# Making the bf16 pieces of a hidden layer inside PSUM, with TensorE doing the subtractions

## The chip, the cores and the metric

The kernel runs on one core of one Trainium2 chip. The metric is the device time of one execution in microseconds (us). Engines are named as in the profile: PE (TensorE matmuls; PEld are its weight loads), DVE (VectorE), ACT (ScalarE), POOL (GpSimd) and SP (SyncE, which issues most DMAs).

## The reference

One layer of a graph network over N = 12500 nodes (32 features: 8 scalars and 8 vectors of 3) and E = 412500 edges, sorted by destination. Cut to what matters:

```
h1 = relu(emb @ fc1_w1 / sqrt(K1)); w  = h1 @ fc1_w2 / sqrt(16)   # K1 = 10 inputs, 16 hidden units, 512 weights per edge
h2 = relu(emb @ fc2_w1 / sqrt(K1)); w2 = h2 @ fc2_w2 / sqrt(16)   # 16 hidden units, 384 weights per edge
s_t, v_t = products of w with x[src], x[dst] and the edge's direction, summed over 16 inputs
scal, gates, vecs = products of w2 with s_t, v_t, summed over 8 or 16 inputs
out = concat(tanh(scal), vecs * tanh(gates)) * norm
x = layernorm(x + segment_sum(out, dst))
```

## The kernel before, in words

An fp32 product is made on TensorE out of bf16 pieces: a number is split into three bf16 pieces (the rounded value, the rounded rest, the rest of that), and six products of pieces are stacked along the contraction. The hidden layer needs this split for each tile: `hid_parts` holds, per edge and layer, the slots 0, 1, 2 (first piece, three times), 3 and 4 (second piece, twice) and 5 (third piece), 16 values each. A DMA transpose (`turn_hid`) brings them into `hid_t`, which is the stationary operand of the products that fill `pw` with edge weights.

The work goes in 403 periods of 1024 edges (8 tiles of 128 edges; the edges of a period stand in 128 partitions by 8 columns). It is a software pipeline written out by hand: in each period every engine runs one body, in a fixed order, on five neighbouring stages called zero (two periods ahead), one, two, three and four. Period by period:

- PE: `fill(two, 1)`, `scalar_sums_turned`, `out_sums(four)` (16 transposes that add up products), `hidden(zero)` (8 matmuls, emb to hidden layer), `fill(two, 2)`, `dst_rows_made(one)` (8 matmuls that pick destination rows), `four_sums_turned` (`gates_t`, `osum_t` turned back), 4 transposes of `vector_sums`, `fill(two, 3)`, the other 20 (`vector_sums_rest`), `fill` 4 and 5, `scalar_sums`, `fill` 6, `scatter`, `vector_sums_turned`, `fill(one, 0)`, `gate_sums`. Seven `fill`s of 8 matmuls each use two halves of `pw` in turn, so a `fill` waits until DVE has multiplied what stood in its half.
- DVE: the products of the weights with node data out of PSUM into `prods`, one after another; between them small steps, `q_first` (line 1386) among them, which waits for ACT's `osum`.
- ACT: copies out of PSUM, the first bf16 pieces, `tanh_out` and `out_sums_back` (`osum`), one-hot rows.
- POOL: eight indirect gathers of source rows per period with small vector steps between them, and the two subtractions of the hidden split, `hid_less_first` and `hid_less_second`.

Each engine's order is fixed by its `body`; the engines wait for each other by semaphores. `hid_ps` (the hidden layer, 256 fp32 columns) and `xd_ps` (destination rows) share the PSUM bank `ph`. Before the change a hidden layer goes PE `hidden` (1015) -> ACT `hidden_out` (787: relu, scaled, into SBUF `hid`) -> ACT `hidden_first` (801) -> POOL `hid_less_first` (643) -> ACT `hidden_second` (807) -> POOL `hid_less_second` (648) -> SP transposes in the next period. No PE instruction waits for any of the pieces except by way of the DMA transposes.

Of the kernel before, what the change touches and what calls it, by code (L numbers as in the profile page):

```python
# [31 lines left out]
def build_gnn_layer(nc, x, src, dst, emb_t, vec, weight, fc1_w1, fc1_w2, fc2_w1, fc2_w2, out):  # L32
# [19 lines left out]
    c1 = 1.0 / (4.0 * 32.0 ** 0.5)  # L52
    c2 = 1.0 / (4.0 * 4.0)
# [42 lines left out]
    with ExitStack() as ctx:  # L96
# [29 lines left out]
        hid = sb("hid", [P, 2 * G, H])  # L126
        hid_rest = sb("hid_rest", [P, 2 * G, H])
# [75 lines left out]
        hid_ps = ph[:, 0:G * 2 * H].rearrange("p (t h) -> p t h", h=2 * H)  # L203
# [58 lines left out]
        hid_done = sem("hid_done")  # L262
        hid_a = sem("hid_a")
        hid_rest_done = sem("hid_rest_done")
# [297 lines left out]
        def _(pool):  # L562
# [13 lines left out]
            nc.gpsimd.tensor_tensor(halves[:, :], identity[:, 0:P // 2], identity[:, P // 2:P], ALU.add).then_inc(s_const, 1)  # L576

# [61 lines left out]
            def hid_less_first(a):  # L639

                pool.wait_ge(hid_a, a.n(1, 1))
                wait(pool, hid_c, a.n())
                nc.gpsimd.tensor_tensor(hid_rest[:, :, :], hid[:, :, :], hid_parts[:, a.par, :, 0:H],
                                        ALU.subtract).then_inc(hid_rest_done, 1)

            def hid_less_second(a):
                pool.wait_ge(hid_b, a.n(1, 1))
                nc.gpsimd.tensor_tensor(hid_parts[:, a.par, :, KH - H:KH], hid_rest[:, :, :],
                                        hid_parts[:, a.par, :, 3 * H:4 * H], ALU.subtract).then_inc(hid_c, 1)

# [26 lines left out]
            def program(is_general):  # L677
                def body(at, i):
# [19 lines left out]
                    if zero is not None:  # L698
                        gathers(zero, 0, (2,))
                        hid_less_first(zero)  # L700
                        gathers(zero, 0, (3,))
                    if three_on is not None:
                        emb_less_second(three_on)
                    if zero is not None:
                        gathers(zero, 0, (4,))
                        hid_less_second(zero)
# [21 lines left out]
        def _(act):  # L728
# [31 lines left out]
            def rows_of(a, side, is_general):  # L760
                if side == 1 and not is_general:
                    act.wait_ge(xd_mm, a.n(1, 1))
                    return xd_ps
# [18 lines left out]
            def hidden_out(a, beside):  # L782
                act.wait_ge(hid_mm, a.n(1, 1))
                if beside is not None:
                    act.wait_ge(xd_mm, beside.n(1, 1))
                wait(act, hid_rest_done, a.n())
                nc.scalar.activation(hid[:, :, :].rearrange("p (l t) h -> p t l h", l=2),
                                     hid_ps.rearrange("p t (l h) -> p t l h", l=2), ACT.Relu,
# [797 lines left out]
```

## Time and profile before

| | us |
|---|---|
| median of 3 runs | 6066.6 |
| lowest and highest | 6059.2, 6067.06 |
| span of the profiled execution, first to last instruction | 6434.2 |

The page of the profile gives for the profiled execution its span alone; no own time beside it is recorded. It is longer than the timed runs by 367.6 us. The busy shares are PE 92%, PEld 88%, DVE 91%, POOL 77%, ACT 62%. A period lasts from one instruction of line 1292 to the next. How to read it: two engines stand above 90%, and the rest of their time is waits for each other, so that the order of events inside one period says more than the shares.

### The profile page before, as it was taken

The page shows a single profiled execution, that of the slowest core. Times are in us where ns is not written, and L with a number is a line of the kernel's source. Part 1 is how long each engine was busy: PE and PEld are TensorE (multiplying, and loading weights), DVE is VectorE, ACT ScalarE, POOL GpSimd, SP SyncE. Part 2 cuts the span into 40 slices and gives each one's busy share as a digit, 9 for nine tenths or more (in the row PEclk, how much of TensorE's full clock was granted, in tenths as well). Part 3 has the DMA queues.
Part 4 walks back from the last instruction along what each step waited for, and adds up shares of the span by engine and source line. Part 5 has one row for each costly group of instructions (what it writes and reads, how often), then busy time and mean ns, then how long its engine had stood idle before and what let it go on. Part 6 is the DMA issues. An engine that isn't in the chain of part 4 may idle for free. (4 is left out here: it accounts for less than half of the span.)

```text
span 6434.2 us, 221220 instructions
## 1 busy us (share of the span) xinstructions
PE 5895.3 (92%) x68616; PEld 5688.0 (88%) x68616; DVE 5884.2 (91%) x7326; ACT 3993.5 (62%) x12507; POOL 4974.7 (77%) x6875
## 2 busy tenths in 40 slices
PE   4999999999999999999999999999999999999997
PEld 3898989889999988988999889889989899999997
DVE  7899999999999998989999989999999899999998
ACT  5666666666666666666666666666666566666663
POOL 6777777777778777877877778777878778787884
PEclk9999999999999999999999999999999999999998
DMA  5444444444444444444444444444444444444442
GB/s 144 89 87 85 88 91 87 86 88 89 87 88 91 86 88 88 89 86 85 92 87 87 87 85 91 86 86 88 92 86 92 85 86 93 86 93 87 92 88 54
DMA packets 1671119, 569.93 MB, mean 89 GB/s; under 512 B 1535146, under 2 KB 1619083, under 8 KB 1670536
## 3 DMA queue, kind: packets, MB, share of 16 engines
q1 hardware_dynamic: 1567911, 516.43, 36.8%
q0 software_dynamic: 103168, 53.03, 6.0%
q8 instruction: 18, 0.29, 0.0%
q14 instruction: 22, 0.18, 0.0%
HBM read 302.19 MB, written 7.26 MB: 48 GB/s over the span
## 5 line engine op out<-in xcount | busy, mean ns | idle before, releaser
L1043 PE MATMUL p<-identity,prods 128*128 128x128 f32 x29016 | 3580.0, 276 | 157.1 <-issue 81.0
L654 POOL DMA_INDIRECT nodes<-x_rows,idx x3224 | 3104.0, 963 | 704.7 <-issue 615.1
L1043 PEld LDWEIGHTS p<-identity,prods 128*128 128x128 f32 x29016 | 3219.4, 143 | 185.0 <-issue 163.6
L1038 PE MATMUL pw<-w_stack,hid_t 128*128 128x128 bf16 x22568 | 1679.3, 220 | 229.6 <-issue 110.8
L1038 PEld LDWEIGHTS pw<-w_stack,hid_t 128*128 128x128 bf16 x22568 | 1435.3, 99 | 316.6 <-issue 138.9
L1292 DVE TENSOR_TENSOR prods<-pw,V 128x2048 f32<-128x2048 f32 x403 | 922.6, 2289 | 177.2 <-remote 83.3
L1337 DVE TENSOR_TENSOR prods<-pw,M 128x1024 f32<-128x1024 f32 x806 | 975.9, 1211 | 15.9 <-issue 6.7
L1347 DVE TENSOR_TENSOR prods<-pw,VT 128x1536 f32<-128x1536 f32 x403 | 704.8, 1749 | 59.7 <-remote 53.2
L870 ACT ACTIVATE off_hot<-node_iota,off_base 128x42 f32<-128x42 f32 x3216 | 747.1, 318 | 0.0
L1314 DVE TENSOR_TENSOR prods<-pw,S 128x1024 f32<-128x1024 f32 x403 | 490.0, 1216 | 84.6 <-PE pw L1038 76.0
L610 POOL TENSOR_TENSOR vr<-V,r 128x384 f32<-128x384 f32 x403 | 347.5, 862 | 244.9 <-issue 185.5
L1322 DVE TENSOR_TENSOR prods<-pw,S 128x1024 f32<-128x1024 f32 x403 | 490.5, 1217 | 11.7 <-PE pw L1038 4.9
L1306 DVE TENSOR_TENSOR prods<-pw,S 128x1024 f32<-128x1024 f32 x403 | 490.5, 1217 | 11.6 <-remote 11.6
L738 ACT ACTIVATE emb_parts<-emb_rest 80x128 bf16<-80x128 f32 x403 | 124.9, 310 | 603.0 <-POOL emb_rest L631 388.0
L1299 DVE TENSOR_TENSOR prods<-pw,V 128x1024 f32<-128x1024 f32 x403 | 489.0, 1213 | 0.0
L1330 DVE TENSOR_REDUCE sv<-prods 128x64 f32<-128x1024 f32 x403 | 486.9, 1208 | 0.0
L751 ACT ACTIVATE off_row<-dstb,row_shift 126x1024 bf16<-126x1024 int32 x403 | 459.3, 1140 | 0.1
L845 ACT ACTIVATE th<-p 128x128 f32<-128x128 f32 x403 | 111.7, 277 | 543.2 <-PE p L1125 538.3
L598 POOL TENSOR_TENSOR msg<-th,late 128x128 f32<-128x128 f32 x403 | 164.0, 407 | 359.4 <-issue 185.0
L757 ACT ACTIVATE hot_t<-off_row 126x1024 bf16<-126x1024 bf16 x403 | 425.4, 1055 | 0.1
L813 ACT ACTIVATE vs_t<-p 128x256 f32<-128x256 f32 x403 | 154.4, 383 | 426.3 <-PE p L1043 339.5
L801 ACT ACTIVATE hid_parts<-hid 128x768 bf16<-128x768 f32 x403 | 347.0, 861 | 0.0
(136 smaller groups left out, 8242.5 us busy)
## 6 DMA issues: line engine op xcount, KB each, us to landing
dstb<-in_dst SPq DMA_DIRECT2D x403, 504.0 KB
nodes<-x_rows,idx POOLq DMA_INDIRECT x3224
emb_stack<-emb_parts SPq DMA_DIRECT2D x2418, 20.0 KB
emb<-in_emb_t SPq DMA_DIRECT2D x403, 40.0 KB
hid_t<-hid_parts SPq DMA_TRANSPOSE x806
idx<-in_src SPq DMA_DIRECT2D x403, 4.0 KB
xw<-x SPq DMA_DIRECT2D x403, 7.9 KB
vecs<-in_vec SPq DMA_DIRECT2D x403, 12.0 KB
```

Of the source, the lines that this page charges most:

```text
L654: nc.gpsimd.indirect_dma_start(nodes[:, p, t, side, :], None, x_rows, bass.IndirectOffsetOnAxis(ap=idx[:, p, side, t:t + 1], axis=0)).then ...
L870: nc.scalar.activation(off_hot[:, t, :], node_iota[:, :], ACT.Square, bias=off_base[:, t:t + 1]).then_inc(off_hot_done, 1)
L1038: mm = nc.tensor.matmul(pw[:, slot, t, :], hid_t[:, layer, a.par, t, :], w2_stack[:, lo:lo + W], start=True, stop=True)
L1043: return nc.tensor.matmul(out, column, identity[:, :], start=first, stop=last, is_transpose=True)
L1292: nc.vector.tensor_tensor(prod_v01.rearrange("p u k t w -> p k t u w"), wts.unsqueeze(1).broadcast_to([P, 2, G, 2 * C, C]), V[:, p, 0:2, : ...
L1299: nc.vector.tensor_tensor(prod_v2.rearrange("p u t w -> p t u w"), wts, V[:, a.par, 2, :, :].unsqueeze(3).broadcast_to([P, G, 2 * C, C]), ...
L1306: nc.vector.tensor_tensor(prod_s[:, :, 0, :, :].rearrange("p u t w -> p t u w"), weights(a, 1, ring).rearrange("p t (u w) -> p t u w", w=C ...
L1314: nc.vector.tensor_tensor(prod_c, weights(a, 2, ring).rearrange("p t (w u) -> p t w u", w=C), S[:, a.par, :, 0:2 * C].unsqueeze(2).broadca ...
L1322: nc.vector.tensor_tensor(prod_s[:, :, 1, :, :].rearrange("p u t w -> p t u w"), weights(a, 3, ring).rearrange("p t (u w) -> p t u w", w=C ...
L1330: nc.vector.tensor_reduce(sv[:, :, :], prod_c, AX.X, ALU.add).then_inc(sv_done, 1)
L1337: nc.vector.tensor_tensor(prod_g[:, :, half, :, :].rearrange("p u t w -> p t u w"), weights(a, 4 + half, ring).rearrange("p t (u w) -> p t ...
L1347: nc.vector.tensor_tensor(prod_o[:, :, 0:3, :, :].rearrange("p u k t w -> p k t u w"), wts.unsqueeze(1).broadcast_to([P, 3, G, C, C]), VT[ ...
```

## The change

The scaled relu output `hid` in SBUF and its rest `hid_rest` are gone. The hidden layer stays in PSUM (`hid_ps`, now ordered by layer and tile) until its three pieces are made:

- ACT `hidden_first` reads PSUM, with relu and a scale of 1 - 2^-8, and writes slots 0 to 2.
- PE `hidden_less(zero, 0)` multiplies slot 0 by minus the identity (`minus_bf`) and adds it to `hid_ps` (one matmul of 256 columns).
- ACT `hidden_second` reads PSUM again, for slots 3 and 4; PE `hidden_less(zero, 1)` subtracts slot 3; ACT `hidden_third` reads what is left, for slot 5.
- POOL's two subtractions go. The factor 1/sqrt(K1) moves into `c1` and `c2`.
- Since a matmul that starts a sum and one that continues it now meet in the bank `ph`, `dst_rows_made(one)` moves ahead of `hidden(zero)` on PE, both wait for `hid_c` of the layer before, and ACT reads `xd_ps` after `hidden` is done: `row_scalars(one, 1)` and `row_vectors(one, 1)` stand right behind `tanh_out`, then `hidden_first`, then `out_sums_back`.

```diff
+            def hid_of(copies):
+                return hid_ps.unsqueeze(2).broadcast_to([P, 2 * G, copies, H])
+            def hidden_first(a):
+                act.wait_ge(hid_mm, a.n(1, 1))
...
+                nc.scalar.activation(parts_of(a)[:, :, 0:3, :], hid_of(3), ACT.Relu, scale=below).then_inc(hid_a, 1)
             def hidden_second(a):
-                act.wait_ge(hid_rest_done, a.n(1, 1))
...
+                act.wait_ge(hid_less, a.n(2, 1))
+                nc.scalar.activation(parts_of(a)[:, :, 3:5, :], hid_of(2), ACT.Relu, scale=below).then_inc(hid_b, 1)
+            def hidden_third(a):
+                act.wait_ge(hid_less, a.n(2, 2))
+                nc.scalar.activation(parts_of(a)[:, :, 5, :], hid_ps, ACT.Relu).then_inc(hid_c, 1)
...
             def hidden(a, is_general):
                 p = a.par
                 pe.wait_ge(stack_in[p], a.k(16 * PIECES))
-                wait(pe, hid_done, a.n())
-                if not is_general:
-                    wait(pe, sv_copied, a.n(4, -6))
+                wait(pe, hid_c, a.n())
...
+            def hidden_less(a, piece, made, is_general):
+                pe.wait_ge(made, a.n(1, 1))
+                slot = (0, 3)[piece]
+                nc.tensor.matmul(hid_ps, minus_bf[:, :], hid_parts[:, a.par, :, slot * H:slot * H + H], start=False,
+                                 stop=True, skip_group_check=True).then_inc(hid_less, 1)
...
                     if two is not None:
                         vector_sums(two, four)
                         pe.wait_ge(pss_done, two.n(1, 1))
                         fill(two, 3, at.par)
+                    if zero is not None:
+                        hidden_less(zero, 0, hid_a, is_general)
+                    if two is not None:
                         vector_sums_rest(two)
...
                         fill(three, 6, at.par)
+                    if zero is not None:
+                        hidden_less(zero, 1, hid_b, is_general)
                     if four is not None:
                         scatter(four, is_general)
```

PE before, from the turned scalar sums (first row) to `fill` 4 and 5 (last row) of one period:

```order
L1092 MATMUL p<-halves,st_t 128x64
L1043 MATMUL p<-identity,prods 128x128 x16
L1015 MATMUL ph<-w_stack,emb_stack 128x32 x8
L1038 MATMUL pw<-w_stack,hid_t 128x128 x8
L1026 MATMUL ph<-xw,hot_t 128x32 x8
L1123 MATMUL p<-identity,gates_t 128x128
L1125 MATMUL p<-identity,osum_t 128x128 x2
L1043 MATMUL p<-identity,prods 128x128 x4
L1038 MATMUL pw<-w_stack,hid_t 128x128 x8
L1043 MATMUL p<-identity,prods 128x128 x20
L1038 MATMUL pw<-w_stack,hid_t 128x128 x16
```

PE now, the same place:

```order
L1079 MATMUL p<-halves,st_t 128x64
L1030 MATMUL p<-identity,prods 128x128 x16
L1013 MATMUL ph<-xw,hot_t 128x32 x8
L994 MATMUL ph<-w_stack,emb_stack 128x2x16 x8
L1025 MATMUL pw<-w_stack,hid_t 128x128 x8
L1110 MATMUL p<-identity,gates_t 128x128
L1112 MATMUL p<-identity,osum_t 128x128 x2
L1030 MATMUL p<-identity,prods 128x128 x4
L1025 MATMUL pw<-w_stack,hid_t 128x128 x8
L1002 MATMUL ph<-hid_parts,minus_bf 128x256
L1030 MATMUL p<-identity,prods 128x128 x20
L1025 MATMUL pw<-w_stack,hid_t 128x128 x16
```

The destination rows (1026, now 1013) went ahead of the hidden layer and of `fill` 2, and the first subtraction (1002) stands between `fill` 3 and the 20 transposes.

ACT before, from `tanh` to the second pieces, with the semaphores that each waits for:

```order
L845 ACTIVATE th<-p 128x128 [waits msg_done,four_back]
L787 ACTIVATE hid<-ph 128x8x2x16 [waits hid_rest_done,xd_mm,hid_mm]
L850 ACTIVATE osum<-p 128x256 [waits msg_done,four_back]
L771 ACTIVATE S<-ph 128x8x8 [waits xd_mm,pc_done,psv_done]
L801 ACTIVATE hid_parts<-hid 128x16x48 [waits turned_in11,turned_in01,hid_done]
L745 ACTIVATE row_shift<-dstb,row_node 126x1 [waits off_row_done,dstb_in1]
L813 ACTIVATE vs_t<-p 128x256 [waits vs_back,vs_sum]
L807 ACTIVATE hid_parts<-hid_rest 128x16x32 [waits hid_rest_done]
```

ACT now, the same place:

```order
L827 ACTIVATE th<-p 128x128 [waits msg_done,four_back]
L758 ACTIVATE S<-ph 128x8x8 [waits xd_mm,hid_mm,pc_done,psv_done]
L364 REGISTER_ALU
L765 ACTIVATE V<-ph 128x24x8 [waits xd_mm,hid_mm,vr_done,pv_done]
L782 ACTIVATE hid_parts<-ph 128x16x48 [waits turned_in11,turned_in01,hid_mm]
L832 ACTIVATE osum<-p 128x256 [waits msg_done,four_back]
L731 ACTIVATE row_shift<-dstb,row_node 126x1 [waits off_row_done,dstb_in1]
L795 ACTIVATE vs_t<-p 128x256 [waits vs_back,vs_sum]
L785 REGISTER_ALU
L786 ACTIVATE hid_parts<-ph 128x16x32 [waits hid_less]
```

`osum`, which stood second behind `tanh`, now stands behind S, V and the first pieces; V came forward from behind the row squares; `hidden_first` is the fourth.

## Rows read from the trace of the kernel before

**Rows 1.** The page, busy time (share of the span) and instructions of each engine.

```profile
PE 5895.3 (92%) x68616; PEld 5688.0 (88%) x68616; DVE 5884.2 (91%) x7326; ACT 3993.5 (62%) x12507; POOL 4974.7 (77%) x6875
```

**Rows 2.** Windows: stretch, busy us (instructions) of each engine, granted clock, DMA.

```profile
3000.00:4500.00 1500.00, 1398.49 (x16316) 1350.78 (x16314) 1380.33 (x1728) 942.26 (x2976) 1176.80 (x1630) 0.99 0.43 88
```

**Rows 3.** Line 1292: count, duration min/median/max in ns, first and last start.

```profile
L1292 DVE TENSOR_TENSOR prods<-pw,V x403: 2272/2292/2293, 83.8 to 6363.8; 128x2048 f32<-128x2048 f32 x135
```

**Rows 4.** Waits, 3000 to 4500 us: us in total, times, longest.

```profile
PE pw L1038 <- DVE prods L1299: 25.8, 47, 1.1
...
DVE p L1386 <- ACT osum L850: 16.9, 44, 1.0
...
ACT th L845 <- PE p L1125: 127.8, 96, 2.0
```

**Rows 5.** Timeline of one period, DVE: start us, us, line and operation.

```profile
4468.84 2.29 DVE L1292 TENSOR_TENSOR prods<-pw,V 128x2048 f32<-128x2048 f32 x1 [0.88 <-remote]
4471.05 1.22 DVE L1299 TENSOR_TENSOR prods<-pw,V 128x1024 f32<-128x1024 f32 x1
...
4474.99 0.35 DVE L1386 TENSOR_TENSOR p<-osum,p 128x192 f32<-128x192 f32 x1
...
4483.36 2.29 DVE L1292 TENSOR_TENSOR prods<-pw,V 128x2048 f32<-128x2048 f32 x1 [0.26 <-PE pw L1038]
```

**Rows 6.** Timeline of the same period, PE matmuls.

```profile
4469.30 1.94 PE L1043 MATMUL p<-identity,prods 128*128 128x128 f32 x16
...
4471.08 0.62 PE L1015 MATMUL ph<-w_stack,emb_stack 96*128 96x32 bf16 x8
...
4472.32 0.62 PE L1038 MATMUL pw<-w_stack,hid_t 128*128 128x128 bf16 x8 [0.62 <-DVE prods L1299]
...
4472.78 0.61 PE L1026 MATMUL ph<-xw,hot_t 126*128 126x32 bf16 x8
4473.24 0.31 PE L1123 MATMUL p<-identity,gates_t 128*128 128x128 f32 x1
...
4474.04 0.61 PE L1038 MATMUL pw<-w_stack,hid_t 128*128 128x128 bf16 x8
4474.48 2.35 PE L1043 MATMUL p<-identity,prods 128*128 128x128 f32 x20
...
4484.16 0.28 PE L1043 MATMUL p<-identity,prods 128*128 128x128 f32 x1
```

**Rows 7.** Timeline of the same period, ACT.

```profile
4473.86 0.28 ACT L845 ACTIVATE th<-p 128x128 f32<-128x128 f32 x1 [1.34 <-PE p L1125]
...
4474.04 0.38 ACT L787 ACTIVATE hid<-ph 128x256 f32<-128x256 f32 x1
...
4474.30 0.39 ACT L850 ACTIVATE osum<-p 128x256 f32<-128x256 f32 x1
...
4474.56 0.25 ACT L771 ACTIVATE S<-ph 128x64 f32<-128x64 f32 x1
4474.67 0.87 ACT L801 ACTIVATE hid_parts<-hid 128x768 bf16<-128x768 f32 x1
...
4481.10 0.32 ACT L778 ACTIVATE V<-ph 128x192 f32<-128x192 f32 x1
...
4481.31 1.05 ACT L757 ACTIVATE hot_t<-off_row 126x1024 bf16<-126x1024 bf16 x1
```

**Rows 8.** Groups by line, 3000 to 4500 us: count, busy us, mean ns, idle before.

```profile
L801 ACT ACTIVATE hid_parts<-hid 128x768 bf16<-128x768 f32 x96 | 82.7, 861 | 0.0
...
L813 ACT ACTIVATE vs_t<-p 128x256 f32<-128x256 f32 x96 | 36.8, 383 | 96.4 <-PE p L1043 78.9 <-issue 17.5
```

**Rows 9.** Groups of POOL by line, the same stretch: its two subtractions.

```profile
L643 POOL TENSOR_TENSOR hid_rest<-hid,hid_parts 128x256 f32<-128x256 f32 x96 | 65.7, 685 | 1.7
L648 POOL TENSOR_TENSOR hid_parts<-hid_rest,hid_parts 128x256 bf16<-128x256 f32 x96 | 65.4, 681 | 2.1 <-issue 0.3
```

More of the change, by code:

```diff
@@ L50, in build_gnn_layer @@
     assert FULL >= 8 and NS <= 512 and SCAN <= 4 and 3 * ER <= ACC
-    c1 = 1.0 / (4.0 * 32.0 ** 0.5)
-    c2 = 1.0 / (4.0 * 4.0)
+    c1 = float(K1) ** -0.5 / (4.0 * 32.0 ** 0.5)
+    c2 = float(K1) ** -0.5 / (4.0 * 4.0)
+    below = 1.0 - 2.0 ** -8
     r3 = 3.0 ** 0.5
@@ L125, in build_gnn_layer @@
         row_node = sb("row_node", [ROWS, 1])
-        hid = sb("hid", [P, 2 * G, H])
-        hid_rest = sb("hid_rest", [P, 2 * G, H])
+        minus_bf = sb("minus_bf", [P, P], BF16)
         hid_parts = sb("hid_parts", [P, 2, 2 * G, KT], BF16)
@@ L780, in row_vectors @@
                                      ).then_inc(sv_copied, 1)
-            def hidden_out(a, beside):
-                act.wait_ge(hid_mm, a.n(1, 1))
[L784 to L788, printed above, removed]
-                                     scale=float(K1) ** -0.5).then_inc(hid_done, 1)
@@ L797, in hidden_first @@
                     wait(act, turned_in[layer][a.par], a.before(2).k(16))
-                if i_first(a):
+                if a.static and a.b * 2 + a.d == 0:
                     act.wait_ge(parts_zero, 1)
-                parts = hid_parts[:, a.par, :, 0:KH].rearrange("p a (g h) -> p a g h", h=H)
-                nc.scalar.activation(parts[:, :, 0:3, :], hid[:, :, :].unsqueeze(2).broadcast_to([P, 2 * G, 3, H]),
-                                     ACT.Copy).then_inc(hid_a, 1)
+                nc.scalar.activation(parts_of(a)[:, :, 0:3, :], hid_of(3), ACT.Relu, scale=below).then_inc(hid_a, 1)
@@ L949, in body @@
                         tanh_out(four)
+                    if one is not None:
+                        row_scalars(one, 1, is_general)
+                        row_vectors(one, 1, is_general)
                     if zero is not None:
-                        hidden_out(zero, None if is_general else one)
+                        hidden_first(zero)
                     if four is not None:
                         out_sums_back(four)
-                    if one is not None:
-                        row_scalars(one, 1, is_general)
-                    if zero is not None:
-                        hidden_first(zero)
                     if turning is not None:
@@ L967, in body @@
                         scalar_sums_out(two)
+                    if zero is not None:
+                        hidden_third(zero)
                     if turning is not None:
                         off_rows(turning)
-                    if one is not None:
-                        row_vectors(one, 1, is_general)
-                    if turning is not None:
                         hot_rows(turning)
@@ L1162, in body @@
                         out_sums(four)
+                    if one is not None and not is_general:
+                        dst_rows_made(one)
                     if zero is not None:
@@ L1167, in body @@
                         fill(two, 2, at.par)
-                    if one is not None and not is_general:
-                        dst_rows_made(one)
                     if four is not None:
@@ L1192, in body @@
                         fill(three, 6, at.par)
+                    if zero is not None:
+                        hidden_less(zero, 1, hid_b, is_general)
                     if four is not None:
```

35 lines of the change are left out of this document (11 added, 24 removed).

## The prediction, made before the changed kernel ran

> **What bounds the kernel now.** I read the page's busy shares first, then one long stretch, then who waits for whom, and last one period in order of time. The shares put PE at 92% and DVE at 91%, POOL at 77%, ACT at 62% [rows 1]: two engines are near their limit, and neither is the one that the change relieves. In the stretch from 3000 to 4500 us there are 96 periods, and DVE is busy 1380.33 us of 1500, which is 14.38 us per period; the clock is granted at 0.99, the full 2.4 GHz level [rows 2]. The first product of a period runs 403 times, from 83.8 to 6363.8 us [rows 3]: 402 periods in 6280.0 us, 15.62 us each in the profiled execution, with 83.8 us ahead and 70.4 us behind (6434.2 - 6363.8). If head and tail are the same without the profiler, the timed 6066.6 us leave 5912.4 us, or 14.71 us a period: 0.33 us above DVE's busy time. I work out a period and add the difference 402 times to the median; the profiled execution's own span would move by the same amount.
>
> The waits say how PE and DVE hold each other. PE waits for the third product of DVE (line 1299) in 47 of 96 periods; DVE waits for ACT's `osum` in 44; ACT waits in all 96, 1.33 us each, for PE's turned sums before `tanh` [rows 4]. For the order I take a period close to the timed ones: 14.52 us from product to product, 4468.84 to 4483.36 [rows 5]. PE starts `hidden` at 4471.08, is through with it some 0.46 us later (8 matmuls like those of the destination rows, 4472.78 to 4473.24), and then stands until DVE's product ends (4471.05 + 1.22 = 4472.27), starting `fill` 2 at 4472.32 with 0.62 us of idle before it [rows 6]. From there it has no gap: `gates_t` is turned at 4473.24, the 20 transposes start at 4474.48, and `out_sums` of the next period at 4484.16 [rows 6]. DVE has no wait at `q_first`: it starts at 4474.99, while ACT's `osum` ends at 4474.30 + 0.39 = 4474.69 [rows 5, 7]. So DVE sets this period, and PE has some 0.6 us to spare, all of it in one place.
>
> **The change part by part.**
> POOL loses two subtractions, 0.685 + 0.681 = 1.37 us a period [rows 9]. POOL is idle nearly a quarter of the time [rows 1], and no engine of the two that bound waits for these pieces within the period. Worth 0. The transposes read the pieces a period later, so a third piece that comes somewhat earlier or later is hidden too.
>
> ACT swaps `hid` (0.38 us) and the first pieces from SBUF (861 ns for 768 elements [rows 8]) for the first pieces from PSUM, and gets a third piece of 256 elements. ACT is busy 62%; its total hardly moves, worth 0. What counts is one duration: `tanh` takes 0.28 us for 128 elements [rows 7] and `vs_t` 383 ns for 256, both out of PSUM [rows 8], 0.83 ns for each further element, so 768 elements give 0.383 + 512 x 0.00083 = 0.81 us. The SBUF row (861 ns) is the upper bound; the bare 768 x 0.83 ns, 0.64 us, the lower. I take 0.81, which goes by the rows that read PSUM.
>
> PE gets two matmuls of 256 bf16 columns. A `fill` of 8 x 128 columns takes 4474.48 - 4474.04 = 0.44 us [rows 6], 0.055 each, so 256 columns are 0.11 us: 0.22 a period. The nearest other rows would say no less than 0.055 each and, if the change of operand costs as much as a whole `fill`, no more than 0.44 each. I take 0.22. The Trainium skill, "TensorE: Matmul & The Clock Gate", Back-to-back issue gap, gives about 81 ns for each load and matmul of 128 columns in a sustained stream. The trace shows 55 ns, and at 81 the 56 matmuls of the seven fills alone would add 56 x 26 = 1.5 us to PE, for which a period of 14.52 us with idle time in it has no room; the sum below goes by the trace.
>
> PE's `dst_rows_made` moves ahead of `fill` 2: 4473.24 - 4472.78 = 0.46 us [rows 6] that now lie in the idle 0.62. By itself that brings `gates_t`, and with it `tanh`, 0.46 us forward, a real gain.
>
> The new wait is the point. `hidden_less(zero, 0)` waits on PE for the first pieces, and behind it in PE's queue stand the 20 transposes and all later fills. ACT makes these pieces only after `tanh`, S and V. From the start of `gates_t` on PE:
> - to `tanh` on ACT: 4473.86 - 4473.24 = 0.62 [rows 6, 7]
> - `tanh` to the next instruction 0.18 (4473.86 to 4474.04), S to the next 0.11 (4474.56 to 4474.67), V to the next 0.21 (4481.10 to 4481.31) [rows 7]
> - first pieces 0.81, and 0.05 from an end to PE's start (4472.27 to 4472.32 [rows 5, 6])
>
> That is 1.98 us, while PE is ready for it after 4474.48 - 4473.24 = 1.24 us [rows 6]. PE stands still for 0.74 us each period, and since `tanh` hangs on PE's own `gates_t`, no shift of PE against the others helps: it is a closed loop. Once round, without any other wait: 1.98; from the 20 transposes to the next `out_sums` 4484.16 - 4474.48 = 9.68; `out_sums` 4471.08 - 4469.30 = 1.78; destination rows and hidden layer 0.46 each; `fill` 2 0.46 (4472.32 to 4472.78); the two subtractions 0.22 [rows 6]. Sum 15.04 us. Where DVE used to set 14.52 us, the loop PE - ACT - PE now does, and DVE gets 0.5 us of waiting.
>
> `osum` moves back behind S, V and the first pieces: its end comes about 0.18 + 0.11 + 0.21 + 0.81 + 0.39 = 1.70 us after `tanh` starts, against 4474.69 - 4473.86 = 0.83 before [rows 7]. The 0.87 us later are partly met by the 0.46 us earlier, and the rest lies inside the slack that DVE gets from the loop. I take 0.
>
> The second subtraction stands behind `fill` 6; its pieces are made well before. ACT's third piece may wait for it by some 0.4 us and push the row squares and the source rows back by 0.5 us; ACT's idle time takes that. I take 0.
>
> Sum: a period of 15.04 us. Against 14.71 timed it is +0.33, if the loop swallows all that now disturbs the timed periods, 133 us in 402 periods; if what lies between 14.52 and 14.71 comes on top again, +0.52, 209 us. The middle, 0.43, gives 173 us. Ends of matmuls are modelled, so PE may be somewhat later than drawn; I add 7 us and say 6247 us, 3% slower. With the costs at their bounds (pieces 0.64 to 0.86, subtractions 0.11 to 0.88 for the two) the loop is 14.76 to 15.75 us; weighed, this case has 6130 to 6370.
>
> **The rivals.**
> *The pieces come in time (faster).* If ACT's pieces reach PE within about 0.2 us of its being ready, the loop stays below 14.5 us and DVE sets the period; `tanh` and `osum` come earlier through the filled gap, and the waits for `osum` (16.9 us in 96 periods [rows 4]) and some behind them vanish. At most the 0.33 us above DVE's busy time goes: 133 us, 5934; I would say 0.2 us, 5986. For it: the 0.62 us gap is real and is filled by the move. Against it: four ACT instructions in a row, each with a row of its own, sum to 1.98 us against 1.24.
>
> *Only work counts (no change).* PE gets 0.22 us and has more than that idle; POOL's relief is worth nothing. The wait at `fill` 2 moves to the first subtraction, and the period stays 14.71: 6067. For it: in total, idle before and after look alike. Against it: 0.74 + 0.22 is more than the 0.62 that goes. The Trainium skill, "Perfetto Trace Analysis", Identifying the Most-Contended Engine, would have the engine of highest occupancy judged and improved first; by that rule a change that frees POOL is worth nothing and one that adds 0.22 us to PE costs at most that. The shares here agree with the first half; the loop is what they don't show.
>
> *DVE is hit at `q_first` (much slower).* If PE does not come forward (its `hidden` waits for the stacked embedding, its `gates_t` for a late `osum_t`), `osum` is a full 0.87 us late in each period, DVE stands for it, and the two loops feed each other: 402 x 0.87 = 350 us, 6417. For it: in 44 of 96 periods DVE already waits there [rows 4]. Against it: the slack of 0.5 us.
>
> **How the numbers follow.** The loop 0.70, in time 0.13, only work 0.07, DVE hit 0.10. What a measurement of this kernel tells from no change is 0.2%, 12 us. The loop and DVE hit are slower for certain, 0.80; in time is faster, 0.13; of only work 0.05 is within 12 us and 0.01 on either side: 0.14 faster, 0.05 the same, 0.81 slower. The range goes from 6075, which leaves the faster cases out with 0.14, to 6390, which leaves 0.08.
>
> **What would show it.** Right: PE idle of 0.6 to 0.8 us before line 1002's first matmul in nearly every period, ended by ACT's `hid_parts`; no idle left before `fill` 2; ACT's `tanh` to the end of the first pieces 1.3 us; DVE idle at `q_first` or at products that wait for a `fill`, its busy time unchanged at 14.38 us; POOL lower by 1.37 us a period. Step wrong: no PE idle at the subtraction (pieces in time); a subtraction that takes 0.3 us or more; `fill` 2 still late. The whole is wrong if the median is at or below 6067.

## The result, and the profile after

The changed kernel takes 6399.0 us (6397.7 to 6400.0) beside 6063.1 us for the kernel before: a ratio of 1.0556, 95% interval 1.0542 to 1.0571, 336 us slower. I had forecast 6247 and a range up to 6390. The direction was right and the size too small.

One thing has to be said of the rows read before: that execution ran with a granted clock of 0.98, its periods lay between 14.2 and 21.5 us, and its span of 6434 us is one that no timed run had. An undisturbed profile of the same kernel, of 6069 us, is in the experiment b0b below; where the two differ, b0b is the one to compare with.

The page of the changed kernel, busy time (share of the span) and instructions [beside rows 1]:

```profile
PE 5915.8 (92%) x69422; PEld 5671.8 (89%) x69422; DVE 5865.3 (92%) x7326; ACT 4041.3 (63%) x12507; POOL 4400.1 (69%) x6070
```

Beside rows 1 the shares of PE and DVE have not moved, and only POOL fell, by what was taken off it. That likeness comes from the disturbed execution: on the page of b0b (below) PE stands at 95% and DVE at 96%, so both fell to 92%. Why they fell the shares do not say; the page's chain of work that ended last, as shares of the span, does:

```profile
PE 50%; ACT 17%; POOL 16%; issue 13%; ACTq 2%; SPq 1%; DVE 1%; DMA 0%; POOLq 0%; DVEq 0%
```

ACT and POOL hold a third of it. The stretch from 3000 to 4500 us [beside rows 2], and the first product of a period over the whole run [beside rows 3]:

```profile
3000.00:4500.00 1500.00, 1413.05 (x16626) 1355.53 (x16624) 1387.12 (x1742) 962.26 (x2998) 1046.95 (x1449) 1.00 0.43 89
```

```profile
L1284 DVE TENSOR_TENSOR prods<-pw,V x403: 2272/2292/2293, 79.9 to 6329.3; 128x2048 f32<-128x2048 f32 x135
```

402 periods in 6249.4 us are 15.55 us each, at the full clock, and 385 of the 402 are between 15.51 and 15.53. So steady a period speaks for a loop that closes, not for a sum of disturbances; the experiments test that. Against 14.71 it is 0.84 us a period, 402 times, the 336 us. The waits of that stretch [beside rows 4], us in total, times, longest:

```profile
POOL vr L610 <- ACT V L765: 264.2, 97, 2.8
...
ACT emb_parts L724 <- POOL emb_rest L631: 182.5, 96, 2.0
...
DVE p L1378 <- ACT osum L832: 76.4, 91, 0.9
...
PE ph L1002 <- ACT hid_parts L782: 59.8, 97, 0.6
...
DVE prods L1284 <- ACT V L765: 31.1, 97, 0.4
PE p L1110 <- ACT osum_t L822: 26.8, 95, 0.3
ACT hid_parts L790 <- PE ph L1002: 17.8, 64, 0.3
```

The wait that I forecast is there, ahead of the first subtraction (line 1002), in each of 97 periods. Beside it stand two that I had not: PE's for `osum_t` (line 1110), and POOL's for ACT's V, 2.7 us long each time (0.3 us in b0b; 1.4 us in p2, where POOL only has less to do, so about half of it is spare time). The groups [beside rows 8]: count, busy us, mean ns, idle before:

```profile
L782 ACT ACTIVATE hid_parts<-ph 128x768 bf16<-128x768 f32 x97 | 78.0, 804 | 0.0
...
L1002 PE MATMUL ph<-hid_parts,minus_bf 128*128 128x256 bf16 x194 | 53.9, 278 | 59.8 <-ACT hid_parts L782 59.8
```

Both new costs were sized well: the first pieces out of PSUM take 804 ns (0.81 forecast), and the subtraction takes PE from 4506.56 to the next matmul at 4506.68, 0.12 us (0.11 forecast; the 278 ns are the pipelined length of one).

One period in order of time [beside rows 5 to 7] shows the two loops. First the end of a period on ACT and what POOL makes of it (start us, us, line and operation, idle before in brackets):

```profile
4499.30 0.45 ACT L765 ACTIVATE V<-nodes 128x192 f32<-128x192 f32 x1
...
4499.83 0.87 POOL L610 TENSOR_TENSOR vr<-V,r 128x384 f32<-128x384 f32 x1 [2.78 <-ACT V L765]
...
4500.84 0.98 POOL L642 DMA_INDIRECT nodes<-x_rows,idx  x1
...
4502.13 0.94 POOL L642 DMA_INDIRECT nodes<-x_rows,idx  x1 [0.30 <-issue]
...
4503.28 0.43 POOL L631 TENSOR_TENSOR emb_rest<-emb,emb_parts 80x128 f32<-80x128 f32 x1
...
4503.75 0.31 ACT L724 ACTIVATE emb_parts<-emb_rest 80x128 bf16<-80x128 f32 x1 [1.80 <-POOL emb_rest L631]
...
4504.07 0.37 ACT L822 ACTIVATE osum_t<-p 128x256 f32<-128x256 f32 x1
...
4504.54 0.30 PE L1110 MATMUL p<-identity,gates_t 128*128 128x128 f32 x1 [0.28 <-ACT osum_t L822]
```

POOL's `vr` waits for V; two gathers, a small step and `emb_rest` stand behind `vr` in POOL's queue; ACT's second piece of the embedding waits for `emb_rest`, with `osum_t` behind it in ACT's queue; and PE's `gates_t` waits for `osum_t`. Then, in the same period:

```profile
4505.09 0.28 ACT L827 ACTIVATE th<-p 128x128 f32<-128x128 f32 x1 [0.66 <-PE p L1112]
...
4505.70 0.80 ACT L782 ACTIVATE hid_parts<-ph 128x768 bf16<-128x768 f32 x1
...
4506.56 0.28 PE L1002 MATMUL ph<-hid_parts,minus_bf 128*128 128x256 bf16 x1 [0.62 <-ACT hid_parts L782]
...
4506.91 0.36 DVE L1378 TENSOR_TENSOR p<-osum,p 128x192 f32<-128x192 f32 x1 [0.89 <-ACT osum L832]
...
4511.95 0.27 PE L1002 MATMUL ph<-hid_parts,minus_bf 128*128 128x256 bf16 x1
4512.26 0.38 ACT L790 ACTIVATE hid_parts<-ph 128x256 bf16<-128x256 f32 x1 [0.28 <-issue]
4512.54 1.14 ACT L737 ACTIVATE off_row<-dstb,row_shift 126x1024 bf16<-126x1024 int32 x1
...
4513.72 1.06 ACT L743 ACTIVATE hot_t<-off_row 126x1024 bf16<-126x1024 bf16 x1
4514.68 0.24 ACT L758 ACTIVATE S<-nodes 128x64 f32<-128x64 f32 x1
4514.82 0.45 ACT L765 ACTIVATE V<-nodes 128x192 f32<-128x192 f32 x1
...
4515.35 0.86 POOL L610 TENSOR_TENSOR vr<-V,r 128x384 f32<-128x384 f32 x1 [2.78 <-ACT V L765]
```

`gates_t`, `tanh`, first pieces, subtraction (4504.54 to 4506.56, 2.02 us; 1.98 forecast) is the piece that both loops share. From there PE needs until 4511.95 to reach the second subtraction; ACT's third piece stands behind it, the row squares and the source rows behind that, and V, the last of them, releases POOL at 4515.35, which is 15.52 us after 4499.83. This is the **long loop**: it takes in the new third piece and POOL's and ACT's queues of the embedding. The **short loop** is the one of the forecast, from `gates_t` through PE's own work back to `gates_t`; without the wait for `osum_t` it would be 15.52 less the distance that this wait adds (PE starts `gates_t` 0.43 us later than `fill` 2's 0.46 us would let it, 4503.65 to 4504.54), 15.09 us.

### The profile page after: what moved, and what is told of

The parts are those of the page before. It is cut to its first block, busy times and chain, and to the rows that moved or that the text cites. A ratio compares the mean times of both kernels' runs of the same rounds, so it can differ in the third digit from the quotient of the medians.

```text
span 6398.2 us, 223408 instructions
## 1 busy us (share of the span) xinstructions
PE 5915.8 (92%) x69422; PEld 5671.8 (89%) x69422; DVE 5865.3 (92%) x7326; ACT 4041.3 (63%) x12507; POOL 4400.1 (69%) x6070
## 4 chain that ended last, share of the span: by engine, by line
PE 50%; ACT 17%; POOL 16%; issue 13%; ACTq 2%; SPq 1%; DVE 1%; DMA 0%; POOLq 0%; DVEq 0%
PE p L1030 30%; PE pw L1025 9%; POOL nodes L642 9%; ACT hid_parts L782 5%; ACT off_row L737 4%; POOL vr L610 3%; POOL emb_rest L631 2%; PE ph L1002 2%; PE p L1117 2%; ACT osum_t L822 2%; PE p L1110 2%; PE p L1060 2%; ACT V L765 2%; POOL r L588 1%; PE p L1112 1%
## 5 line engine op out<-in xcount | busy, mean ns | idle before, releaser
L1030 PE MATMUL p<-identity,prods 128*128 128x128 f32 x29016 | 3508.3, 273 | 1.2 <-ACT vs_t L795 0.6
L1025 PE MATMUL pw<-w_stack,hid_t 128*128 128x128 bf16 x22568 | 1655.9, 219 | 7.1 <-DVE prods L1291 3.7
L1025 PEld LDWEIGHTS pw<-w_stack,hid_t 128*128 128x128 bf16 x22568 | 1454.2, 99 | 27.3 <-DVE prods L1291 4.1
L1002 PE MATMUL ph<-hid_parts,minus_bf 128*128 128x256 bf16 x806 | 224.6, 279 | 267.4 <-ACT hid_parts L782 266.0
L1378 DVE TENSOR_TENSOR p<-osum,p 128x192 f32<-128x192 f32 x403 | 146.1, 363 | 341.9 <-ACT osum L832 320.3
L1002 PEld LDWEIGHTS ph<-hid_parts,minus_bf 128*128 128x128 bf16 x806 | 78.1, 97 | 336.4 <-ACT hid_parts L782 334.5
```

The costliest lines, as they stand in the source:

```text
L1025: mm = nc.tensor.matmul(pw[:, slot, t, :], hid_t[:, layer, a.par, t, :], w2_stack[:, lo:lo + W], start=True, stop=True)
L1030: return nc.tensor.matmul(out, column, identity[:, :], start=first, stop=last, is_transpose=True)
```

## The experiments

Each is one short edit, or several of them together. Times are medians of several runs (b0 and b0b are one run each), ratios against the kernel before, timed beside it. "Period" is the mean distance of the first products.

**x1_third_late: the changed kernel, third piece behind the source rows.**

```diff
-                    if zero is not None:
-                        hidden_third(zero)
...
                         row_vectors(one, 0, is_general)
+                    if zero is not None:
+                        hidden_third(zero)
```

> The changed kernel with ACT's hidden_third moved behind the source rows' row_vectors, nothing else. Theory A (two closed loops: a short one PE gates_t - ACT tanh, S, V, first pieces - PE, 15.09 us a period, and a long one that goes on through the second subtraction, ACT's third pieces, the row squares, the source rows, POOL's vr and two gathers, emb_rest, ACT's emb and osum_t back to PE's gates_t, 15.52 us): the long loop gets about 0.5 us shorter, the short one sets the period at 15.1 us, 6225 us (6205 to 6250), and PE's idle time before gates_t (0.28 us a period) goes. Theory B (PE's own work plus the first subtraction's wait is simply more than drawn): unchanged, 6390 to 6405. Theory C (DVE's wait for osum sets it): unchanged, 6390 to 6405.

Measured: 6211.6 us, ratio 1.0244 (1.0227 to 1.0262), period 15.08. One instruction of 0.38 us, moved, is worth 187 us. The wait for `osum_t` is gone and the waits for V and `emb_rest` are shorter, while the wait at the subtraction stands as it was. The waits in the same stretch:

```profile
POOL vr L610 <- ACT V L765: 205.5, 99, 2.2
...
ACT emb_parts L724 <- POOL emb_rest L631: 123.8, 100, 1.4
```

**x2_pool_early: the changed kernel, the embedding's first subtraction ahead of POOL's first gather.** It cuts the long loop at another place.

```diff
                     windows, more = (NW, 1) if is_general else (1, 0)
+                    if three_on is not None:
+                        emb_less_first(three_on)
```

(and the call is gone from its old place)

> The changed kernel with POOL's emb_less_first moved ahead of the period's first gather, nothing else. Theory A: the long loop is cut by more than 1 us on POOL, so the short loop sets the period at 15.1 us: 6225 us (6205 to 6250), as for the third pieces moved. Theories B and C: nothing on PE, ACT or DVE is changed, 6390 to 6405.

Measured: 6226.8 us, 1.0268 (1.0251 to 1.0285), period 15.11. Two cuts at different places, on ACT and on POOL, each take away some 0.4 us a period and end at the same 15.1: one long loop goes through both, and something of 15.1 us is left.

**x6_third_pool: both cuts.**

> The changed kernel with the third pieces moved behind the source rows and POOL's emb_less_first moved ahead. Theory A: each alone has already left the short loop as the bound (15.08 and 15.11 us), so both together bring nothing more: 6195 to 6220. Theory B' (each cut its own part of one long chain, and the rest of that chain is what is left): the parts add up, 6030 to 6100.

Measured: 6224.5 us, 1.0267 (1.0249 to 1.0284), period 15.10. The second cut adds nothing; the time is even 13 us above that of x1 alone and 4.5 us above the range I gave. PE's waits in this stretch are those at the first subtraction (61.2 us in 99 periods) and 1.6 us of others, and ACT's `tanh` waits for PE in each of 100 periods: PE waits for ACT and ACT for PE. This is the short loop by itself, and it is what my forecast described: 15.04 us by my sum.

**x3_less_late: the changed kernel, the first subtraction behind the 20 transposes on PE.** It opens the short loop at the wait.

```diff
                         fill(two, 3, at.par)
+                        vector_sums_rest(two)
                     if zero is not None:
                         hidden_less(zero, 0, hid_a, is_general)
-                    if two is not None:
-                        vector_sums_rest(two)
```

> The changed kernel with PE's first subtraction behind the 20 transposes instead of ahead of them. Theory A: PE's wait there (0.6 us a period) and the short loop are gone, the long loop gets about 0.9 us shorter on PE and some 0.2 longer on ACT, 14.7 to 14.9 us a period, 6060 to 6140 us. Theory B: PE gets 0.6 us back, 6140 to 6170. Theory C: osum is as late as it was, 6350 to 6405.

Measured: 6213.1 us, 1.0248 (1.0231 to 1.0265), period 15.08: I expected 6060 to 6140. PE no longer waits at the subtraction, but it still waits for `osum_t` ahead of `gates_t`, 0.29 us a period. One period shows by which way the loop closes now:

```profile
3500.36 0.36 DVE L1377 TENSOR_TENSOR p<-osum,p 128x192 f32<-128x192 f32 x1 [0.82 <-ACT osum L832]
...
3504.52 0.62 PE L1025 MATMUL pw<-w_stack,hid_t 128*128 128x128 bf16 x8 [0.17 <-DVE prods L1328]
...
3505.28 0.38 ACT L790 ACTIVATE hid_parts<-ph 128x256 bf16<-128x256 f32 x1 [0.63 <-PE ph L1002]
...
3513.08 0.30 PE L1110 MATMUL p<-identity,gates_t 128*128 128x128 f32 x1 [0.29 <-ACT osum_t L822]
```

DVE waits for `osum` (in all 100 periods) and then for nothing up to the product of line 1328; PE's `fill` 6 waits for that product (in 49 of 100), the second subtraction stands behind `fill` 6, ACT's third piece waits for it, and from there the way is the long loop's. So the long loop stays without PE's wait at the first subtraction, in half of the periods by way of DVE and `osum`. That it ends at 15.08 like x1 is a coincidence as far as the runs show.

**x4_act_early: the changed kernel, S, V and the first pieces ahead of `tanh` on ACT.** It shortens what both loops share.

```diff
                         out_sums_out(four)
-                        tanh_out(four)
                     if one is not None:
                         row_scalars(one, 1, is_general)
                         row_vectors(one, 1, is_general)
                     if zero is not None:
                         hidden_first(zero)
                     if four is not None:
+                        tanh_out(four)
                         out_sums_back(four)
```

> The changed kernel with ACT's S, V and first pieces ahead of tanh instead of behind it. Theory A: the first pieces no longer hang on PE's gates_t, the short loop is gone and the long one is 0.9 us shorter, 14.6 us; DVE with 14.38 us of work sets the period, 14.5 to 14.7 us, 5980 to 6060 us. Theory B: PE gets 0.6 us back, 6140 to 6170. Theory C: osum comes 0.8 us earlier, the wait of DVE for it goes, 6050 to 6090.

Measured: 6129.8 us, 1.0107 (1.0090 to 1.0124), period 14.87; PE's wait at the subtraction is left in 12 of 101 periods. 269 us come back, but not all: 5980 to 6060 was missed. PE still waits ahead of `gates_t` in 98 periods, 0.28 us each (17.4 us in 62 of them for `osum_t`, 10.2 us in 36 without a name in the trace), so the long loop is probably what is left. By an estimate from the changed kernel's rows it is 15.52 - 0.62 = 14.90 us without the wait at the subtraction.

**x5_all: the three moves x1, x2 and x4 together.**

> The changed kernel with three moves at once: ACT's S, V and first pieces ahead of tanh, its third pieces behind the source rows, POOL's emb_less_first ahead of the first gather. Theory A (two closed loops): both are cut, the long one by some 1.8 us more than by the first move alone (14.87 us a period there, with PE still waiting 0.28 us for osum_t); DVE with 14.38 us of work sets the period at 14.5 to 14.6 us: 5980 to 6020 us, faster than the kernel before. Theory B (what is left over the kernel before is PE's added work, 0.2 to 0.3 us a period): 6100 to 6130.

Measured: 6069.9 us, 1.0014 (1.0004 to 1.0023), period 14.72. Missed (5980 to 6020): with both loops shortened the kernel stops at the time of the kernel before, though half of its periods take 14.29 us or less. It also runs into a new wait: ACT's first pieces wait for the DMA transposes that read the buffer, 32.1 us in 40 of 102 periods.

**p1_swap: the kernel before, only the destination rows moved ahead of `hidden`.** The part of the change that I had called a real gain.

> The kernel before with dst_rows_made ahead of hidden on PE, as the change has it, and nothing else of the change. Theory A: this is the good part of the change; PE's idle time before fill 2 is filled and gates_t comes 0.46 us earlier, DVE waits less for osum: 5990 to 6050. Rival: DVE is bound by its own 14.38 us and the waits lie elsewhere, 6055 to 6070.

Measured: 6067.8 us, 1.0007 (0.9997 to 1.0016). Nothing. PE waits ahead of `hidden` for the DMA of the stacked embedding, 46.1 us in 51 periods. It does so in the undisturbed kernel before as well (47.0 us in 64, b0b below), and there `fill` 2 has no wait at all in the same stretch: the idle 0.62 us that the move was to fill belonged to the disturbed execution.

**p2_no_pool: the kernel before without POOL's two subtractions.** The second pieces are made of the hidden layer itself and the third stay zero, so the split is left out.

> The kernel before without POOL's two subtractions; ACT's second pieces are made from the hidden layer itself and the third pieces stay zero (this part of the computation is left out). It prices POOL's relief alone. Theory A: nothing waits for POOL there, 6050 to 6070. Rival (POOL's queue delays emb_rest or the messages): 0.1 to 0.3 us a period, 5940 to 6030.

Measured: 6059.9 us, 0.9996 (0.9987 to 1.0006). What the change takes off POOL is worth nothing, as forecast.

Three kernels, p1, p2 and x5, differ in much and have the same 14.72 us. In each, SyncE hardly ever waits (0.5, 15.1 and 1.4 us of 1500): it issues DMAs one after another all the time. The next experiments test whether that is the bound. The first three ran on another chip: the kernel before itself took 6467 us there, with a granted clock of 0.976.

**b0_before, b1_late_on_act, x7_all_late_on_act (the other chip).**

> The kernel before itself, profiled again, since its first profiled execution ran 6434 us of span with a clock of 0.98 and periods scattered from 14.4 to 21 us. Theory Q: the kernel before is bound by SyncE's queue of DMA issues. The version with all three reorderings spends on SyncE, per period, about 12.6 us inside issues and their register work and 2.05 us in the 0.03 to 0.06 us between them, 14.67 in all, and its period is 14.72. Q expects here: time 6055 to 6070, period 14.70 to 14.74, no wait of SyncE longer than 0.1 us in most periods (the gap ahead of the load of idx at its 0.04 us), and DVE and PE each idle for 0.2 to 0.6 us a period. Rival D: the kernel before is bound by DVE's work, 14.38 us a period, and disturbances make the rest. D expects DVE idle below 0.1 us a period, and SyncE waiting for some 0.3 us or more in most periods.

> The kernel before, with the three small loads late_dst, late_base and late issued by ACT, ahead of vs_t, where ACT idles for 1.2 us, in place of SyncE. SyncE loses 3 issues of 0.33 to 0.38 us with their register work and gaps, about 1.3 us a period; nothing else is changed. Theory Q (SyncE's queue sets 14.67): the period falls to what DVE and PE want, 14.3 to 14.5 us, so 402 x 0.2 to 0.4 = 80 to 160 us off: 5905 to 5985, and SyncE then waits for about 1 us a period. Rival D (DVE's 14.38 and disturbances): 6055 to 6070, as before. Rival L: the three issues on ACT run past vs_t and push the second pieces back, so the kernel is slower than before, 6080 to 6200.

> The changed kernel with all three reorderings (first pieces of the next edges ahead of the tanh, third pieces behind the row vectors, the first subtraction of the embedding ahead of the first gather), which gave 6070, and with the three small loads late_dst, late_base and late issued by ACT in place of SyncE. Theory Q: the third bound was SyncE's 14.67 us a period; without it the bound is PE's busy 14.39 or the short loop of 15.08 shortened by the tanh's and sum's 0.7 us, about 14.4: period 14.3 to 14.5, 5900 to 5985. Rival M: the 14.7 is a mean over the short loop's quick and late turns, and SyncE only happens to be full: 6050 to 6075, as with the three reorderings alone. Rival L: ACT's three issues, 1.1 us, lie in the loop: 6090 or more.

Measured: 6486.8 us (one run), 6506.8 us with ratio 1.0061 (1.0028 to 1.0095), and 7386.1 us with ratio 1.1416 (1.1362 to 1.1471). In all three PE stands still for one to several us at a time (a stop of 1 us or more comes 25 times a millisecond in b0, 32 in b1 and 50 in x7). In b0 and b1 most of that is put down to ACT's `gates_t` (68.9 us in 31 waits in b0), which itself waits for something the trace calls remote; in x7 most has no name. They tell the theories apart in nothing. x7's 18 us a period came on this chip alone (x7b below), and its cause stays open: DVE waits there ahead of the gate products, 216.9 us in 111 waits, for something the trace does not name.

The next four had a chip with a clock of 0.996 again, and 6066.4 us for the kernel before.

**b0b_before: the kernel before, profiled again.**

> The kernel before itself, one look beside the next three, for the waits of SyncE. On a chip that holds TensorE's clock at 0.996, as in the first eight experiments: theory Q (SyncE's queue of issues is full) expects 6055 to 6070, and SyncE idle for less than 0.15 us of a period in gaps over 0.1 us (it was 0.22 in the versions that ran at 14.72, twice 0.11 for the two calls' worth of a register read). Rival D (DVE's 14.38 is the bound, disturbances the rest) expects SyncE idle for 0.3 us or more. On a chip like the last one, which held 0.976 and stopped TensorE for up to 3.8 us at a time, 6440 to 6490 and no verdict.

Measured: 6068.9 us, period 14.71. The page's busy shares and its chain of work that ended last:

```profile
PE 5753.4 (95%) x68616; PEld 5584.4 (92%) x68616; DVE 5852.2 (96%) x7326; ACT 3945.6 (65%) x12507; POOL 4967.1 (82%) x6875
...
SPq 39%; PE 23%; issue 15%; DMA 7%; DVE 6%; ACT 5%; POOL 4%; DVEq 1%; ACTq 0%; POOLq 0%
```

SyncE's queue (SPq) has no busy share, but it holds the largest part of the chain. One whole period of SyncE's queue, from one load of the weights to the next:

```profile
3512.82 0.33 SPq L497 DMA_DIRECT2D late<-in_weight  x1
3513.25 4.90 SPq L415 DMA_DIRECT2D emb_stack<-emb_parts  x6
3518.36 1.26 SPq L426 DMA_TRANSPOSE hid_t<-hid_parts  x1
3519.83 0.86 SPq L407 DMA_DIRECT2D emb<-in_emb_t  x1
3520.89 0.36 SPq L434 DMA_DIRECT2D idx<-in_src  x1
3522.23 0.39 SPq L442 DMA_DIRECT2D dstb<-in_dst  x1
3522.82 0.33 SPq L444 DMA_DIRECT2D xw<-x  x1
3523.36 1.30 SPq L426 DMA_TRANSPOSE hid_t<-hid_parts  x1
3524.86 0.43 SPq L467 DMA_DIRECT2D vecs<-in_vec  x1
3525.40 0.38 SPq L473 DMA_DIRECT2D inv_near<-inverse_rows  x1
3525.97 0.33 SPq L490 DMA_DIRECT2D late_dst<-in_dst  x1
3526.39 0.38 SPq L492 DMA_DIRECT2D late_base<-in_dst  x1
3526.95 0.33 SPq L497 DMA_DIRECT2D late<-in_weight  x1
```

14.13 us from first to last row, of which the issues up to the last row are 11.25 and the rest is register reads (one of 0.46 us among them) and arithmetic, semaphores and gaps of 0.03 to 0.06 us between instructions; no row has a wait. (Every second period has the jump back of the loop and more register work in it; the next one here takes 15.25 us. The mean of all periods is 14.71.) What it does wait for, and what PE waits for, in 3000 to 4500 us:

```profile
SPq L497 <- DVE msg L1396: 14.2, 43, 0.4
```

```profile
PE ph L1015 <- DMA emb_stack<-emb_parts: 47.0, 64, 1.2
```

SyncE waits 14.2 us of 1500, 0.14 a period, and PE waits 47.0 us for what SyncE issues. DVE is idle 0.38 us a period, so it is not the bound that I had taken it for. (Q's and D's marks were for SyncE's gaps of over 0.1 us. They come to 0.2 us a period, nearly all at the jump back, between Q's 0.15 and D's 0.3; the next two experiments decide.)

**b1b_late_on_act: the kernel before, three small loads issued by ACT.** Their code is unchanged, only its engine and place:

```diff
 SyncE:
-                    if two is not None:
-                        load_destinations(two, is_general)
-                    if three is not None:
-                        load_weights(three)
 ACT:
                     if turning is not None:
                         row_shifts(turning)
+                    if two is not None:
+                        load_destinations(two, is_general)
+                    if three is not None:
+                        load_weights(three)
                     if two is not None:
                         vector_sums_out(two)
```

> The kernel before with the three small loads late_dst, late_base and late issued by ACT ahead of vs_t, a second time: the last chip held only 0.976 to 0.98 of the clock, stopped TensorE for 1 to 3.8 us some 35 times a millisecond and gave 6507 beside 6467, on which neither theory is told apart. On a chip with a clock of 0.996: theory Q: SyncE loses about 1.3 us a period of issues, the period falls from 14.72 to 14.3 to 14.5, 5905 to 5985. Rival D: 6055 to 6070. Rival L (the issues on ACT delay vs_t): 6080 to 6200.

Measured: 5888.4 us, ratio 0.9709 (0.9693 to 0.9725), 2.9% faster than the kernel before, the fastest of all here and below the range I gave. The windows, the first products, SyncE's waits and the chain that ended last:

```profile
3000.00:4500.00 1500.00, 1495.22 (x17918) 1464.12 (x17916) 1495.36 (x1896) 1022.66 (x3268) 1288.61 (x1793) 1.00 0.46 96
```

```profile
L1292 DVE TENSOR_TENSOR prods<-pw,V x403: 2268/2272/2292, 82.7 to 5816.9; 128x2048 f32<-128x2048 f32 x135
```

```profile
SPq L434 <- DMA nodes<-x_rows,idx: 78.8, 106, 1.1
SPq L415 <- POOL emb_parts L617: 38.9, 74, 1.6
...
PE 50%; POOL 4%; issue 2%; ACT 1%; DVE 1%; ACTq 0%; POOLq 0%; DVEq 0%
```

Now DVE and PE are busy for over 1495 of 1500 us, three quarters of the periods take 14.17 or 14.18 us, SyncE waits, it is gone from the chain, and PE's wait for the stacked embedding is gone from the stretch. The bound of the kernel before was SyncE's queue. These 14.2 us, not the 14.38 that I had taken, are also what DVE needs.

**b2_double_late: the kernel before, with one more 4 KB load in SyncE's queue.**

```diff
                 sp.dma_start(late[:, p, :], ...).then_inc(wgt_in[p], 16)
+                sp.dma_start(late_more[:, p, :], ...).then_inc(wgt_in[p], 16)
```

(and POOL's wait for the weights counts both loads)

> The kernel before, where SyncE issues the 4 KB load of the weights twice, the second into a tile that nothing reads: one more issue of 0.33 us with about 0.1 us of registers and gaps around it, and 4 KB of 1380 KB more to move. Theory Q (SyncE's queue is full, every issue is paid): 0.37 to 0.45 us a period, 150 to 180 us more, 6210 to 6245. Rival D (DVE is the bound, SyncE has room): 6060 to 6070.

Measured: 6206.7 us, 1.0231 (1.0213 to 1.0248): 140 us for a load that nothing uses, 0.35 us a period, just under the range I gave. The granted clock was 0.988 in these runs, 0.996 beside it; but SyncE waits only 10.7 us of 1500, PE's wait for the stacked embedding grows to 67.4 us, and SyncE's queue holds 58% of the chain in place of 39%. Adding an issue and taking issues away agree.

**x7b_all_late_on_act: x5_all with the three loads on ACT.**

> The three reorderings and the small loads on ACT, a second time, for the same reason (the last chip gave 7386 with a period of 18, DVE waiting for 2.9 us of each ahead of the gate products, and a clock of 0.959). On a chip with a clock of 0.996: theory Q: 5900 to 5985, period 14.3 to 14.5. Rival M (the 14.7 is the mean over the short loop's quick and late turns): 6050 to 6075. Rival S (the 18 us come from the order itself, with whatever chip): over 6800.

Measured: 5934.3 us, 0.9786 (0.9769 to 0.9802), period 14.38. The last bound of x5 was SyncE's as well. But it is 46 us slower than b1b, which has none of the change in it: even with its loops shortened the change brings nothing.

**a1_late_on_act: the changed kernel as it is, with the three loads on ACT.**

> The changed kernel as it is, with the three small loads late_dst, late_base and late issued by ACT ahead of vs_t. In the kernel before that gave 5888 in place of 6066, since SyncE's queue was its bound. Theory A (the changed kernel is bound by the long way round: third pieces, source rows, POOL's gathers, embedding, osum_t, gates_t, 15.52 us): SyncE waits there for about 1 us a period already, so nothing comes of it: 6390 to 6410, period 15.5 to 15.55. Rival Q' (SyncE's lateness still feeds the long way, by the idx load ahead of the gathers): 6250 to 6350. Rival L (the issues delay ACT's chain): above 6430.

Measured: 6400.9 us, 1.0557 (1.0540 to 1.0575). SyncE has spare time there and more of it is worth nothing. So the price of the change, with SyncE's queue out of the way on both sides, is 6400.9 - 5888.4 = 512 us, of which a full queue had hidden 175.

## Why the prediction was right or wrong

**The closed loop PE, ACT, PE: right, and well sized.** "The loop PE - ACT - PE now does" set the period, at 15.04 us; alone (x6) it takes 15.10. PE's wait at the subtraction is 0.62 us for 0.74 forecast, in each period, and `gates_t` to the subtraction takes 2.02 us for 1.98. The first pieces (0.80 for 0.81), the subtraction (0.12 for 0.11) and POOL at nothing (p2) held.

**The third piece: the step that failed, a term put at 0.** I wrote: "ACT's third piece may wait for it by some 0.4 us and push the row squares and the source rows back by 0.5 us; ACT's idle time takes that. I take 0." The wait was there (0.28 us in the period shown) and the push as well. The cover was not: ACT's idle time lies ahead of `vs_t`, `emb_parts` and `tanh`, and between the third piece and V there is none, as the timeline from 4512.26 to 4514.82 shows. V then releases POOL, and through POOL's gathers and the embedding ACT's `osum_t` and PE's `gates_t`, which begins the same loop again. Its true size is the 0.43 us a period, 174 us, between the two loops (6399.0 for the changed kernel, 6224.5 for the short loop in x6). Moving that one instruction gives 187 us back (x1), and cutting the same loop on POOL gives 172 (x2). POOL's idle share had told me that it had time; it waits 2.7 us ahead of `vr` and is late all the same.

**`osum` at 0: right here, with a larger wait than forecast.** DVE waits 0.8 us a period for it, where I had given the loop's slack as 0.5 (0.3 us in b0b). It costs nothing in the changed kernel: in the stretch from 3000 to 4500 us PE has no wait for DVE. In x1 the wait stands and the time falls. In x3, with the first subtraction out of the way, it does become a link of the loop. No experiment took it away by itself.

**The filled gap: wrong, and without effect on the sum.** "A real gain" was worth nothing (p1). The gap ahead of `fill` 2 was read rightly from rows 6, but it belongs to that execution: in b0b PE waits ahead of `hidden` instead, for the stacked embedding, and the move does not bring that forward.

**What bounds the kernel before: wrong.** I put the 0.33 us between DVE's 14.38 and the timed 14.71 down to disturbances and DVE's waits. It was SyncE's queue, which the page leaves out of its busy shares, and DVE's own need is 14.2 us (b1b). For the forecast that did little harm, since the loop replaces whatever bound there was; I had added 0.10 us a period for those "disturbances" and 7 us for the ends of matmuls. Without both, 14.71 to 15.04 gives 6199, and the short loop alone measured 6224.5. That 6247 lies near 6224.5 is thus partly luck: the 47 us added stood for things that no run shows in the changed kernel, and happened to cover the 0.06 us a period by which the loop was summed too short.

**The rivals.** *In time* and *only work counts* are out: PE waits at the subtraction in every period. *DVE is hit at `q_first`* came near in time (6417) and wrong in mechanism: with the wait for `osum` still there, x1 runs at 6212.

## What to carry to other kernels

When an instruction is put into an in-order queue, list everything behind it up to the next wait on each engine, and follow what the last of these releases until it comes back to the start; idle time covers a delay only where it lies between the new instruction and the one that is waited for. Read the queue that issues the DMAs as an engine of its own: one that never waits may be the bound, even where the page shows no busy share for it; the page's chain names it, and taking an issue away or adding one settles it. Read all this from an execution whose span fits the timed runs: a disturbed one shows gaps that are not there. And a kernel held by such a queue hides gains and losses elsewhere, so undo the bound before judging an edit.

## What the runs showed of the hardware

- In the period of b0b shown, an issue costs SyncE 0.33 to 0.43 us for most loads (0.38 for 0.5 KB, 0.39 for 504 KB), 0.86 us for the embedding's 40 KB, 0.82 us for each piece of the stacked embedding (4.90 us for 6), and 1.26 to 1.30 us for a DMA transpose. One small load with what surrounds it cost the kernel 0.35 us a period (b2); three moved to ACT's queue freed 0.44 us a period, until PE and DVE were full (b1b).
- ACT issues DMAs beside its own work: in a period of b1b (from 3503.58 us) the three issues take 0.37 to 0.47 us each, and two of them begin while an activation is still running.
- The same kernel took 6062 to 6066 us on four chips and 6467 on a fifth, where the granted clock was 0.976. The kernel of x7 took 5934 us on one of the four (as x7b, 2% faster than the kernel before) and 7386 on the fifth (14% slower). Why, no run shows. An order tuned on one chip need not be ahead on the next.
